# Transposing the rows of FFN 8 and FFN 9 by DRAM scratch and VectorE instead of TensorE

## The reference, cut to what matters

```python
x = x + 0.5 * ffn(layernorm(x))
x = x + attention(layernorm(x))
x = x + 0.5 * ffn(layernorm(x))

def ffn(x):                        # x_prev: the row before; zero for the first of a sequence
    xr = mu_r * x + (1 - mu_r) * x_prev
    xk = mu_k * x + (1 - mu_k) * x_prev
    return sigmoid(xr @ W_r) * (square(relu(xk @ W_k)) @ W_v)

def attention(x):                  # 16 heads of 16
    q, k = relu(x @ Wq.T) / 4, relu(x @ Wk.T) / 4
    kv = k.T @ (x @ Wv.T)          # per head, over a whole sequence
    o = q @ kv
    return (o / rms(o per head) * silu(x @ Wu.T)) @ Wo.T
```

## Time and profile before

| | |
|---|---|
| median of 3 runs | 306.08 us (305.85 to 307.25) |
| profiled execution | 305.79 us, of which the span from the first to the last instruction is 304.0 us |
| granted TensorE clock over the span | 0.999 of full |
| busy, VectorE | 248.2 us (82%) |
| busy, ScalarE | 236.1 us (78%) |
| busy, GpSimd | 210.6 us (69%) |

### The profile page before, as it was taken

The page is one execution under the profiler, slowest core; times in us unless marked ns, Lnnn a source line. Parts: engine busy times, 40 slices in busy tenths (PEclk is TensorE's granted clock), DMA queues, the critical chain, the costliest instruction groups (busy, mean ns, idle before and its releaser), DMA issues.

```text
span 304.0 us, 5770 instructions
## 1 busy us (share of the span) xinstructions
PE 296.4 (97%) x1995; PEld 270.9 (89%) x1995; DVE 248.2 (82%) x605; ACT 236.1 (78%) x462; POOL 210.6 (69%) x236
## 2 busy tenths in 40 slices
PE   6999999999999999999999999999999999999995
PEld 5888889988998999898988998999999999999894
DVE  4899996776976876969992998687988888999695
ACT  3988959969779589599178267489797979699981
POOL 4598969689489478567377117636797979759923
PEclk9999999999999999999999999999999999999999
DMA  6960040130210400400000000000010101002123
GB/s 205 381 245 1 1 140 0 34 106 0 72 70 0 140 0 2 138 1 2 0 3 0 0 2 0 2 2 2 0 40 32 55 18 67 4 0 72 46 94 138
DMA packets 17472, 16.09 MB, mean 53 GB/s; under 512 B 802, under 2 KB 16164, under 8 KB 17444
## 3 DMA queue, kind: packets, MB, share of 16 engines
q1 hardware_dynamic: 17152, 15.47, 15.3%
q10 hardware_dynamic: 292, 0.26, 0.3%
HBM read 8.91 MB, written 6.82 MB: 52 GB/s over the span
## 4 chain that ended last, share of the span: by engine, by line
PE 74%; DVE 16%; ACT 5%; issue 2%; DMA 1%; POOL 1%; ACTq 1%; DVEq 0%
PE psK L1363 7%; PE psK L1365 7%; PE psK L1364 7%; PE psX L1363 7%; PE psX L1365 7%; PE psX L1364 7%; PE psRV L1363 6%; PE psRV L1365 6%; PE psRV L1364 6%; DVE mix L1002 4%; PE psA L1568 2%; PE psX L1581 2%; PE psK L1568 2%; PE psX L1495 2%; PE psA L1380 2%
## 5 line engine op out<-in xcount | busy, mean ns | idle before, releaser
L1002 DVE SCALAR_TENSOR_TENSOR mix<-psA,mu,mix 128x512 f32<-128x512 f32 x60 | 41.7, 745 | 10.3 <-ACT mix L683 10.3
L466 POOL TENSOR_TENSOR mix_k_lo<-mix,mix_k_hi 128x512 fp32r<-128x512 f32 x26 | 33.7, 1315 | 5.4 <-ACT mix_k_hi L716 5.4
L683 ACT ACTIVATE mix<-psA,one_mu 128x511 f32<-128x511 f32 x60 | 36.9, 697 | 0.0
L1363 PE MATMUL psRV<-ffn_hi,mix_r_hi 128*128 128x256 f32 x120 | 34.3, 286 | 0.0
L1365 PE MATMUL psRV<-ffn_hi,mix_r_lo 128*128 128x256 f32 x120 | 33.6, 280 | 0.0
L1364 PE MATMUL psRV<-ffn_lo,mix_r_hi 128*128 128x256 f32 x120 | 33.5, 279 | 0.0
L666 ACT ACTIVATE xn<-xs,shiftA,rstdA 128x256 f32<-128x256 f32 x53 | 27.9, 627 | 1.9 <-POOL shiftA L450 1.9
L1363 PE MATMUL psRV<-ffn_hi,act_hi 128*128 128x256 f32 x96 | 27.4, 286 | 0.0
L1364 PE MATMUL psRV<-ffn_lo,act_hi 128*128 128x256 f32 x96 | 26.8, 279 | 0.0
L1365 PE MATMUL psRV<-ffn_hi,act_lo 128*128 128x256 f32 x96 | 26.8, 279 | 0.0
L971 DVE BATCH_NORM_STATS2 statsA<-xs 128x6 f32<-128x256 f32 x64 | 22.5, 416 | 2.3 <-DMA xs<-x_dram 2.2
(11 more groups left out here) (213 smaller groups left out, 1094.0 us busy)
## 6 DMA issues: line engine op xcount, KB each, us to landing
xs<-x_dram SPq DMA_DIRECT2D x7, 512.0 KB, 7.8
out_dram<-xs SPq DMA_DIRECT2D x7, 512.0 KB, 2.8
spread<-xn SPq DMA_DIRECT2D x10, 256.0 KB, 3.0
squares<-spread SPq DMA_DIRECT2D x8, 256.0 KB, 2.7
wsum<-spread SPq DMA_DIRECT2D x2, 256.0 KB, 2.9
out_dram<-xs SPq DMA_DIRECT2D x4, 128.0 KB, 1.7
xs<-x_dram SPq DMA_DIRECT2D x2, 128.0 KB, 2.6
xs<-x_dram ACTq DMA_DIRECT2D x2, 128.0 KB, 2.8
```

Source lines behind the costliest of these rows:

```text
L466: nc.gpsimd.tensor_tensor(mix_k_lo[:, h, :], mix[:, 0, h, :], mix_k_hi[:, h, :].bitcast(F32), ALU.subtract).then_inc(s_lo_k, 1)
L683: nc.scalar.activation(mix[:, rk, h, 1:BLOCK], psA[:, h, 0:BLOCK - 1], ACT.Copy, scale=one_mu[:, rk, h:h + 1]).then_inc(s_prev, 1)
L1002: nc.vector.scalar_tensor_tensor(out=m, in0=psA[:, h, :], scalar=mu[:, rk, h:h + 1], in1=m, op0=ALU.mult, op1=ALU.add).then_inc(s_mix, 1)
L1363: nc.tensor.matmul(dst, a_hi, b_hi, start=start, stop=False)
```

## The change

FFN 8 and 9 join `TURNED`. `transpose_a(8)` and `transpose_a(9)` leave PE; `turn(8)` enters DVE's list behind `gate_heads(2)`, `turn(9)` behind `head_norms(3)`; SP issues two writes and two reads more for each. On DVE the Newton steps of block 2 move from ahead of `x2_low(7)` to behind `mix_current(8)` and two of the four `silu(7, t)`. On ACT `mix_high(8, 0)` moves behind `keep_g_rows(2)`, and `normalize(9)` ahead of `relu_q(7)`. POOL's list stays as it is.

```diff
-        TURNED = range(3, 8)
+        TURNED = range(3, 10)
@@ ACT
             x1_high(7)
-            mix_high(8, 0)
             sigmoid_u(7, 0)
 ...
             keep_g_rows(2)
+            mix_high(8, 0)
             mix_high(8, 1)
             square_heads(3)
+            normalize(9)
             relu_q(7)
-            normalize(9)
@@ DVE
             gate_heads(2)
-            head_norms(2)
+            turn(8, [(s_gu, 6)])
+            for g in range(2):
+                head_sums(2, g)
             x2_low(7)
             keep_g(6)
             mix_current(8)
+            silu(7, 0)
+            silu(7, 1)
+            head_norms(2, True)
+            silu(7, 2)
+            silu(7, 3)
             stats_a(9)
-            projections(7)
             g_low(2)
@@ DVE, in the loop over n from 8
                 head_norms(j, n > 8)
+                if n == 8:
+                    turn(9, [(s_gu, 8)])
                 mix_current(n + 1, (0,))
@@ PE
             q_of(6, (s_x2, 4))
-            transpose_a(8, [(s_gu, 6)])
             transpose_b(7)
@@ PE, in the loop over n from 8
                 ffn_r(n)
-                transpose_a(n + 1, [(s_gu, 8)])
+                if n > 8:
+                    transpose_a(n + 1, [(s_gu, 8)])
                 transpose_g(j, ...)
```

## The result

The changed kernel takes 308.70 us in the median of 10 runs (306.95 to 309.45), the kernel before beside it 305.96 (10 runs); the ratio is 1.0062, 95% interval 1.0039 to 1.0085: slower, by about 0.6%. The profiled execution took 306.95 us, with a span of 305.2.

A forecast was written before the change was run, and what follows sets the result against it. PE, 97% busy, was taken to bound FFN 8's place, but ACT, DVE and POOL FFN 9's. Late k_lo (+1.73) less ACT's gain (0.09) on 305.79 gave 307.43, forecast with offset as 307.6 us, range 305.5 to 308.8.

The forecast's parts named there:

- Step 1: FFN 8 on PE: without transpose_a(8), PE waits for ACT's relu of q, so gram(6) starts only 0.32 us earlier.
- Step 2: Newton steps on DVE, behind keep_g(6), mixes and two silu: begin at 185.9 instead of 177.50, end at 188.2.
- Step 3: POOL's queue: norm_second(2), then k_lo, wait for the late Newton steps; third tile of gram(7) on PE 1.73 us later.
- Step 4: FFN 9: its chain runs as before, 1.64 us later; transpose_a(9)'s 0.87 us becomes PE waits before transpose_g(3) and transpose_g(4).
- One sign of step 4: In FFN 9, PE's transpose_g(4) would wait for POOL's gout for over a microsecond.
- The 0.09 gain from the rows ahead of the relu: ACT in FFN 9: normalize(9) ahead of relu_q(7) removes ACT's lateness of about 0.1 us; counted as 0.09.
- the margin: FFN 9: turn(9) on DVE is just in time for ACT's previous(9), with 0.15 us to spare.
- The sum: Whole kernel: profiled execution 305.79 + 1.73 - 0.09 = 307.43 us; 307.7 with the 0.29 offset, stated as 307.6.
- The gain that passes: Rival: Newton steps and k_lo in time, PE the bound at both places; 304.05 us, or 304.3 with offset; chance 0.08.
- The late turn: Rival: turn(9) on the path at FFN 9, slower still by up to a turn's 1.4 us, to 309.1; chance 0.11.
- only the heads are late: Rival: the wait ends with transpose_g(2), k_lo costs little more; 0.4 to 1.1 us later, 306.2 to 307.2; chance 0.13.
- the likeliest case: Steps 1 to 4 together, 1.64 us later; own range 306.8 to 308.2 us; chance 0.61.

The follow-up runs named there:

- klo_split: Changed kernel with the first half of kt_low(7) ahead of norm_second(2) on POOL, the second half behind it; 307.91 us median, stage time 148.22.
- ffn8_alone: Changed kernel with transpose_a(9) back on PE and turn(9) taken out, so only FFN 8's rows are turned; 308.62 us median, stage time 148.35.
- ffn9_alone: Kernel before with only FFN 9's rows turned and normalized ahead of the relu, Newton steps as before; 305.82 us median, stage time 147.04.
- newton_early: Changed kernel with block 2's Newton steps between x2_low(7) and keep_g(6) on DVE, four silu behind the mixes; 305.39 us median, stage time 146.46.
- adds_last_clock_up: newton_early with FFN 9 to 11's statistics behind head_norms, add_ffn2(n - 1) behind r_low(n + 1), six dummy transposes at the start; 306.84 us, stage time 147.73.

## Why the prediction was right

The mechanism was right at every step, the sizes nearly so. The median, though, came out 1.1 us above the predicted 307.6, for a reason that the prediction didn't contain, and 0.1 us inside the end of its range (308.8): that it stayed inside is luck.

- **Step 1**, the gain at `gram(6)` was put at 0.32 us instead of 0.87. Measured: 178.26 + 0.11 against 178.85, 0.48. I had PE start 0.15 us behind ACT's relu; it starts 0.05 behind.
- **Step 2**, first Newton step at 185.9: measured 185.47, `head_rn` to 187.73 against 188.2. Some 0.3 of the 0.4 is the trace's offset and step 1's error; that the steps run straight behind the mixes and two `silu` was right.
- **Step 3**, the one that decides: POOL's `gout` from 188.26 predicted, 187.81 measured, its 1.56 us right (1.57), the last `k_lo` to 192.36 predicted, 191.86 measured. `project_out(2)` is 1.36 us later than before, not 1.73: the term was too large by the nearly 0.4 us that steps 1 and 2 handed on. The klo_split run shows what the step left out: when the two run at once, GpSimd's `k_lo` holds VectorE's head steps up.
- **Step 4**, the chain at FFN 9 follows and the 0.87 us become waits: confirmed by ffn8_alone and ffn9_alone, whose stage times are within 0.1 us of what they edit, and by the 0.9 to 1.0 us that come free at `attend(5)` when DVE's path is made shorter. One sign of step 4 failed: PE was to wait for POOL's `gout` in `transpose_g(4)` for over a microsecond, and its marked waits there are 0.34 us, for DVE's half, and 0.20, for POOL's. The 0.09 gain from the rows ahead of the relu: 0.1 in ffn9_alone, which carries the whole of FFN 9's change. Normalizing in the permuted order took 2.07 us for FFN 8's four instructions, as before. `turn(9)` ran from 205.69 to 207.12 and ACT's `previous(9)` from 206.99, behind its own sigmoid; the margin held.
- **The sum** 305.79 + 1.64: the profiled execution was 306.95, 1.16 more; by the stage time 1.3.
- **The median** is at 308.70 because six of ten executions fell in the longer group. The prediction took the 0.29 us between one execution and the median as an offset and had no term for the start.
- **Rivals.** The gain that passes needs Newton steps in time, as said; newton_early gives it at `gram(7)`, and then 146.46 shows that the 1.74 us still don't all pass. The late turn was not what happened. Nor was "only the heads are late", though its 306.2 to 307.2 holds the profiled 306.95 as well as the likeliest case's 306.8 to 308.2 does: the number can't tell the two apart, the 0.66 and 0.24 us that PE waits for `k_lo` do.

## What to carry to other kernels

Before a step is moved back on one engine, read who waits for it on an in-order engine and what is queued behind that wait there: here the Newton steps ended 9.4 us before PE's next use of them, but with 1.57 us of `gout` and 2.52 us of `k_lo` behind them on POOL they had only 6.8 us to spare (190.7 less these two, less 179.8), and were moved by 8. A saving on the busiest engine is worth what the next chain leaves of it; find the places where that engine waits, however short, since these say that its work isn't the bound: in rows 9 it is the second half of `transpose_g(4)`, which goes on only when POOL's `gout` has ended. When a wait is taken away, state what is late next before the run; five of the kernels here failed on that, and adds_last_clock_up repeated the fifth.

## What the runs showed of the hardware

- Small VectorE instructions on SBUF (0.2 us) that started while a GpSimd instruction on 128x512 elements with two SBUF inputs was under way ended just behind it: 0.55 to 1.31 us in the rows above. Beside an idle GpSimd, or one at work on 128x4 elements, the same instructions took 0.19 to 0.26 us. VectorE's batch statistics (0.41 us) and PSUM reads (0.74) were not held, so they are the cheaper thing to leave in such a stretch.
- The first products of an execution took 379 ns in one execution and up to 631 in another of the same program, 2 us of the whole, at a granted clock of 1.00 in both, and six dummy transposes in PE's first gaps made that rare. A handful of runs can't tell two kernels apart by 0.5% while it is there; the time from a common later point can.
